# Narrower selections in a graph network's edge loop: 4 to 13 destination columns a slot in place of 6 to 13

## What is computed

```python
def _L0_gnn_ref(x, bases, w_comp, h_bias, norm, src, dst, etype):
    weight = jnp.einsum('rb,bio->rio', w_comp, bases)      # 32 relations of 8 bases
    h_rel = jnp.einsum('ni,rio->rno', x, weight)
    msg = h_rel[etype, src] * norm
    return jax.ops.segment_sum(msg, dst, num_segments=n_nodes) + h_bias

def _L1_gnn_ref(x, edge_index, W, b):                      # self loops are added to row, col
    deg = segment_sum(ones, row); dis = rsqrt(deg)
    h = x @ W.T + b
    return relu(segment_sum((dis[row] * dis[col])[:, None] * h[row], col))

h = jnp.maximum(_layernorm(x), 0.0)
x = x + _L0_gnn_ref(h, bases, w_comp, h_bias, edge_weight, src, dst, edge_type)
h = jnp.maximum(_layernorm(x), 0.0)
x = x + _L1_gnn_ref(h, edge_index, W, b)
```

## Time and profile before

| | us |
|---|---|
| median of 3 runs | 593.65 (590.59 to 594.00) |
| profiled execution, its own time | 594.36 |
| its span, first to last instruction | 592.6 |
| PE busy | 497.5 (84%) |
| POOL busy | 354.1 (60%) |
| DVE busy | 345.0 (58%) |
| ACT busy | 155.3 (26%) |

### The profile page before, as it was taken

The page is one execution under the profiler, slowest core; times in us unless marked ns, Lnnn a source line. Parts: engine busy times, 40 slices in busy tenths (PEclk is TensorE's granted clock), DMA queues, the critical chain, the costliest instruction groups (busy, mean ns, idle before and its releaser), DMA issues.

```text
span 592.6 us, 16039 instructions
## 1 busy us (share of the span) xinstructions
PE 497.5 (84%) x5873; PEld 318.2 (54%) x5873; DVE 345.0 (58%) x999; ACT 155.3 (26%) x280; POOL 354.1 (60%) x476
## 2 busy tenths in 40 slices
PE   3140667899999899999999998998989998999973
PEld 1020655555666556666656665655656565665530
DVE  8994674577855356857766765654566324242036
ACT  3682552364202122212320320320233101131020
POOL 3535657367776776766757767767767777730000
PEclk9665667899999999999999999998989999999995
DMA  8798969566787887886866968878967888845006
GB/s 275 248 358 287 369 213 335 178 175 176 209 259 216 258 259 206 256 254 173 276 208 178 281 181 231 276 207 243 270 204 227 261 239 253 241 147 160 0 21 156
DMA packets 51861, 132.84 MB, mean 224 GB/s; under 512 B 11775, under 2 KB 17776, under 8 KB 51702
## 3 DMA queue, kind: packets, MB, share of 16 engines
q0 software_dynamic: 27040, 99.60, 55.6%
q1 hardware_dynamic: 23788, 30.99, 16.7%
q10 hardware_dynamic: 954, 1.13, 0.6%
HBM read 123.14 MB, written 11.10 MB: 227 GB/s over the span
## 4 chain that ended last, share of the span: by engine, by line
PE 70%; DVE 11%; DMA 9%; issue 4%; ACT 2%; POOL 1%; SPq 1%; DVEq 0%; ACTq 0%
PE PS L1754 28%; PE PS L1722 21%; DMA gath<-rows_layer,srcs 7%; PE PS L1795 7%; PE PS L1746 5%; PE PS L1774 4%; DMA types_by_slot<-h_t 1%; PE PS L1730 1%; POOL gath L805 1%; PE PS L1589 1%; DVE room_b L1558 1%; PE PS L1763 1%; DVE gath L1572 1%; DVE stats L1076 1%; ACT room_b L951 1%
## 5 line engine op out<-in xcount | busy, mean ns | idle before, releaser
L805 POOL DMA_INDIRECT gath<-rows_layer,srcs x335 | 334.3, 998 | 154.7 <-PE PS L1730 83.3
L1722 PE MATMUL PS<-sel,gath 128*128 128x48 f16 (+7 forms) x4020 | 303.3, 205 | 28.8 <-issue 12.0
L1722 PEld LDWEIGHTS PS<-sel,gath 128*128 128x128 f16 x4020 | 241.8, 102 | 154.8 <-issue 64.5
L1754 PE MATMUL PS<-room_b,zt 128*128 128x512 f16 x384 | 127.7, 383 | 0.4 <-issue 0.3
L1754 PE MATMUL PS<-room_b 128*128 128x512 f16 (+1 forms) x384 | 117.1, 382 | 0.5 <-DMA gath<-rows_layer,srcs 0.4
L1730 PE MATMUL PS<-oh_ad,gath 128*128 128x30 bf16 (+7 forms) x335 | 64.6, 193 | 1.9 <-DVE c_i L1369 1.9
L1795 PE MATMUL PS<-u_t,room_c 128*128 128x512 f16 (+2 forms) x200 | 57.1, 395 | 6.3 <-issue 3.8
L874 ACT CAST val<-val_f 128x64 f16<-128x64 f32 x42 | 11.0, 262 | 176.9 <-DVE val_f L1246 176.9
L1277 DVE TENSOR_TENSOR masks<-iota_n,dloc 128x24 bf16<-128x24 f32 (+12 forms) x92 | 18.0, 196 | 62.5 <-issue 33.2
L1754 PEld LDWEIGHTS PS<-room_b 128*128 128x128 f16 (+1 forms) x384 | 38.4, 105 | 12.9 <-DMA gath<-rows_layer,srcs 0.5
L1283 DVE TENSOR_TENSOR sel<-masks,val 128x192 f32<-128x192 bf16 (+12 forms) x92 | 38.6, 420 | 0.0
(11 more groups left out here) (245 smaller groups left out, 505.3 us busy)
## 6 DMA issues: line engine op xcount, KB each, us to landing
room_b<-in_L_gnn_bases_dram SPq DMA_DIRECT2D x8, 1024.0 KB, 11.0
gath<-rows_layer,srcs POOLq DMA_INDIRECT x335
x_base<-in_x_dram SPq DMA_DIRECT2D x5, 500.0 KB, 5.5
x_t<-x_base SPq DMA_DIRECT2D x19, 128.0 KB
u_t<-in_x_dram SPq DMA_DIRECT2D x9, 256.0 KB, 6.0
types<-types_by_slot SPq DMA_DIRECT2D x144, 16.0 KB
x_layer<-x_t SPq DMA_DIRECT2D x18, 128.0 KB, 4.2
gath<-x_layer SPq DMA_DIRECT2D x18, 128.0 KB, 2.7
```

What stands on the lines that cost most here:

```text
L805: pool.indirect_dma_start(out=gath[:, s % UN, :], out_offset=None, in_=tab0_d[:, :], in_offset=bass.IndirectOffsetOnAxis(ap=srcs[:, s:s + ...
L1722: last = mm(there, gath[:, s % UN, D * t + P * f:D * t + P * (f + 1)], sel_parts[:, here, k, 0:NB * w, u], start=first and t == 0 and u == ...
L1754: last = mm(PS[0:r, PBANK[q], :], zt[q][:, t, f, b, 0:r], base_hl[:, b, u, f, :], start=(m == 0), stop=(m == NM - 1))
```

## The change

WIN is computed by another formula. Before, it was 3 columns plus 1.2 times the columns that 128 edges fill on average at the tile's upper end. Now it is 1 plus the columns that a larger number of edges fills on average, where that number, 181.96, is the count whose mean less four deviations (four square roots) is 128.

```diff
     SLOTS = [-(-int(E * share(i) + 2.0 * math.sqrt(E * share(i) * (1 - share(i)))) // P) for i in TORDER]
-    WIN = [min(TN, 3 + math.ceil(1.2 * P * 2 * math.sqrt(N * min(TN * (i + 1), N)) / E)) for i in TORDER]
+    def window_of(i):
+
+        per_column = E / (2 * math.sqrt(N * min(TN * (i + 1), N)))
+        edges = ((4 + math.sqrt(16 + 4 * P)) / 2) ** 2
+        return min(TN, 1 + math.ceil(edges / per_column))
+
+    WIN = [window_of(i) for i in TORDER]
     S0 = [sum(SLOTS[:r]) for r in range(NTI)]
```

## The result

The changed kernel takes 587.0 us as the median of 7 runs (585.17 to 589.46); the kernel before, run beside it, 591.48 us (590.59 to 594.0). The ratio is 0.9925, with a 95% interval of 0.9905 to 0.9944: 4.4 us or 0.75% faster. Measured once more on another occasion the ratio was 0.9938 (0.9914 to 0.9961). The forecast was 588.0 us, 0.95% under the 593.65 us known then. Where a ratio stands, executions more than 1.5% above the fastest of the same kernel are left out, which here concerns only the experiment with fewer gathers (five of twelve).

A forecast was written before the change was run, and what follows sets the result against it. Two coupled chains, POOL's gathers and PE, tied by a ring of eight buffers, bound the kernel; savings of 1.6, 1.0, 0 and 3.7 us made 6.3, from 594.36 to 588.1, said as 588.0 us; range 585.5 to 590.5.

The forecast's parts named there:

- The columns' price: Edge matmuls: 32 columns cost 26 ns, 40 columns 27 ns; narrower widths save PE 10 us in all.
- The rival of a fixed price below 56 columns: Edge matmuls under 56 columns cost a fixed time, so tiles 0, 1 and 2 give nothing: 590.5 us, chance 0.10.
- PE as the bound up to slot 62: Tiles 2 to 4, 100 to 157 us: PE is the bound, so 1.6 us of saving pass on whole.
- The middle: 157 to 437 us: of 3.0 us left after moved products, a third passes on, 1.0 us (bounds 0 and 3.0).
- The last long tile: Tile 0, 437 to 530 us: gathers set the pace, so nothing passes on (bounds -1.2 and +1.5).
- The end: After the last slot: 26 early matmuls left in place of 43, 3.7 us less, no new wait at the flush.
- The sum: Whole kernel: 6.3 us less than the profiled 594.36 us gives 588.1, forecast as 588.0 us.
- PE as the bound throughout: Whole kernel: all of the 10 to 11.6 us saved on PE arrive, 584 us; chance 0.15.
- The gather chain that swallows the end too: Loop and end: only the early 1.6 us and little else stay, 591 to 592.5 us; chance 0.22.
- Slower by waits at product starts: Products begun earlier run into waits for their inputs, holding PE and everything behind: some 600 us, chance 0.06.
- The slow loop: Edges spanning more columns than their window send the whole kernel to its loop, over 15,000 us; chance 0.01.

The follow-up runs named there:

- e1: New widths everywhere, products placed as computed from the old widths, against the kernel before: 0.9956, 589.09 us.
- e4: Kernel before with new widths in the first five tiles alone (slots 0 to 62), old placing of products: 0.9995 of the kernel before.
- e9: The changed kernel itself, unaltered, run again beside the late plan on one chip: 0.9938 of the kernel before.
- e2: Kernel before with old widths, but products placed as with the new ones: 1.003 of the kernel before, 593.14 us.
- e12: Changed kernel with the planner counting new widths up to place 13 of the tile order, old ones from 14 on: 0.9987 of the kernel before.
- e8: As the late plan, but the planner takes 2 columns for the last long tile, leaving 18 early matmuls: 0.9983 of the kernel before, 591.14 us.
- e6: Gathers of 64 rows in place of 128 from slot 8 on, new widths, old placing of products: 0.9758 of the kernel before.
- e5: Kernel before with gathers of 64 rows in place of 128 from slot 8 on, old widths: 0.9857 of the kernel before.
- the late plan: Changed kernel with the planner counting old widths up to place 13 of the tile order, new ones from 14 on: 0.9908 and 0.9911 of the kernel before.

## Why the prediction was right, and where it wasn't

**The columns' price: right.** The forecast had 25.4 to 29.1 ns as bounds for 32 columns and took 26; it is 25.5. The rival of a fixed price below 56 columns is out: 48 columns took 29.1 ns before. The 8.9 us less of busy time fit the 10 us. The floor of about 25 ns from start to start that the Trainium skill gives ("TensorE: Matmul & The Clock Gate", section "Wait — 56ns, not 53.3ns?") for 32 columns holds in this trace.

**PE as the bound up to slot 62: about right.** 1.6 us were forecast; slot 62 is reached at 155.6 to 157.2 us with new widths and at 157.5 to 157.8 with old ones (leaving out the profiled execution of before), some 1 us in the mean.

**The middle: right in its sum by two errors.** I let a third of 3.0 us pass, 1.0 us in all. Measured, the loop from 62 to 334 gains nothing (372.2 and 370.8 us against 371.1), but not because the gathers swallow it. The narrower matmuls alone gain 2.5 to 3.5 us there (e1 against e4 and before; 2.6 us for the whole kernel by its median), more than the third that I let pass. The moved products take it back, and more than their own work: I charged those that pass out of the end into the loop with 0.216 us each, and those that only move within it, at slots 83 to 128, with nothing. The latter cost 1.6 us up to slot 139 in e9 and 2.7 us in e2, neither with a fall of the clock there; the 3.5 and 3.7 us of the change's own trace and of e12 hold 1.7 us of clock. The step that failed is the count of moved products as mere work. What counted was where PE stands at a tile's end: 1.35 us more of standstill at slot 113's gather, and at slot 128 too few products left to cover the flush. Where both lie could have been read from the plan that I had worked through. I had named the right measure, POOL's real standstill, but only as something that shrinks.

**The last long tile: right.** Nothing passes either way (99.5 and 99.8 us against 100.0), with 1.19 us a slot, forecast 1.20. e8 shows from the other side how near the edge is, and e6 that the narrow widths pay there once the gathers are quicker.

**The end: right, and slightly larger.** 26 matmuls left, no new wait at the flush; 56.1 and 56.9 us behind slot 334 against 60.2 to 61.5 for the kernels with 43 left, so 4 to 5 us for a forecast 3.7.

**The sum.** -6.3 forecast, -4.4 measured (-3.7 the second time). I also started from too high a time: the shown execution of before stood 3 us late at slot 62, and the median of the first three runs, 593.65 us, lies 2.2 us over that of seven. The start of 594.36 us was too high by 2.9 us and the gain too large by 1.9, so that 588.0 lies within 1.0 us of 587.0 is in part luck.

**The rivals.** PE as the bound throughout (584 us) is out by e1, and by e5 and e6, where cheaper gathers changed what PE's saving was worth. The gather chain that swallows the end too is out, since the end came through whole. Slower by waits at product starts is out, as the kernel got faster; but a relative of this rival was real, products moved away from or ahead of boundaries, worth some 1.6 to 2.7 us and not 8. The slow loop was not entered: no time comes near its 15,000 us. (That figure is itself a low bound, as the 64 records of L1746 are 32 matmuls, at 1.18 us each.)

## What to carry to other kernels

When two engines feed each other through a ring, count the time that the faster one really stands still, without its fixed handover, and ask of each edit what it does to that number; busy shares of 96% hide it. A planner that prices work shares in every change of a size: take the two apart, since here the size gave some 3 us in the loop, and the plan took 1.6 to 2.7 us of it back and gave 4 us at the end. Extra work put between slots is free only below the partner's pace (1.19 of 1.25 us); here it cost most just ahead of a tile's end, and where it was taken away from a tile's end. Before a difference of 2 us between two traces is put down to the program, compare the granted clock over the same stretch.

The best version measured is the late plan, 0.991 of before on both occasions; it differs from the change by less than this measurement can tell for certain.

## What the runs showed that I had not expected

- An indirect gather of 64 rows takes POOL 0.90 us, one of 128 rows 0.95 us, each with 0.30 us to the next: nearly all of the price is the instruction's.
- Halving the rows gathered (DMA share 0.78 to 0.47) gave 1.4%, with a pace that was only 0.05 us quicker.
- The granted clock can fall to its lower level for a few us within the loop, at a place that changes from one execution to the next; a fall in slots 130 to 132 cost 1.7 us, one in slots 31 and 32 1.6 us. In the change the one at 251 us came right behind PE's waits for the flush of slot 128, but e9 and e2 had the same waits and kept the higher clock until slot 139.
